# Attention stage of a four-layer graph network: another layout, ring depth and engine for the split values, masks computed in an earlier stage

## The reference

```python
h = x @ W
x_i = h[dst]; x_j = h[src]
alpha = x_i @ wa[:c] + edge_attr @ wa[c:c + ce] + x_j @ wa[c + ce:]
alpha = where(alpha > 0, alpha, 0.2 * alpha)
m = segment_max(alpha, dst)
a = exp(alpha - m[dst])
a = a / (segment_sum(a, dst)[dst] + 1e-16)
out = segment_sum(a[:, None] * x_j, dst) + bias
```

## Time and profile before

| | before |
|---|---|
| median of the runs | 3592.72 us |
| profiled execution | 3591.77 us, span 3590.0 us |
| PE, busy | 2911.7 us, 81% |
| VectorE (DVE), busy | 2904.2 us, 81% |
| ScalarE (ACT), busy | 2219.8 us, 62% |
| GpSimd (POOL), busy | 1584.4 us, 44% |
| stage of the passes | about 1241 to 1712 us of the span |
| attention stage | from about 2682 us; values from 2721.0 to 3571.6 us |
| last instruction group | output stores at 3582 us |

### The profile page before, as it was taken

How to read it: one execution, slowest core, us unless ns; L and a number is a source line. 1 busy time by engine, 2 the same in 40 slices (tenths; PEclk the granted TensorE clock), 3 DMA queues, 4 the chain that set the end, 5 groups by cost and what they waited for, 6 DMA issues and landing times.

```text
span 3590.0 us, 122167 instructions
## 1 busy us (share of the span) xinstructions
PE 2911.7 (81%) x50473; PEld 2637.4 (73%) x50473; DVE 2904.2 (81%) x4610; ACT 2219.8 (62%) x6003; POOL 1584.4 (44%) x1253
## 2 busy tenths in 40 slices
PE   0199999999999699899688888787768888888886
PEld 0178888888888599899677777777757777777775
DVE  7599999999999522233688888898857999999997
ACT  6334444444444400001698888898857898899887
POOL 2012222222221000000399988898964655666564
PEclk9999999999999899999899999999977888888887
DMA  8157777777777799898687877787738888888884
GB/s 221 66 157 244 237 232 234 243 237 231 234 243 236 253 370 360 330 328 320 215 279 259 264 264 248 254 271 250 257 124 302 279 278 277 276 290 274 267 278 129
DMA packets 606666, 907.43 MB, mean 253 GB/s; under 512 B 358505, under 2 KB 494858, under 8 KB 587163
## 3 DMA queue, kind: packets, MB, share of 16 engines
q1 hardware_dynamic: 583992, 800.62, 68.1%
q10 hardware_dynamic: 19763, 94.38, 7.1%
q0 software_dynamic: 2352, 4.52, 0.3%
HBM read 651.96 MB, written 247.40 MB: 251 GB/s over the span
## 4 chain that ended last, share of the span: by engine, by line
PE 36%; DVE 27%; ACT 14%; issue 10%; POOL 6%; DMA 5%; ACTq 1%; SPq 0%; DVEq 0%; POOLq 0%
PE ps L683 9%; PE ps L1047 8%; PE ps L709 4%; DMA U<-AD 4%; ACT U L1627 3%; POOL EDG L1268 3%; DVE EDG L1755 3%; DVE U L1817 3%; PE ps L696 3%; ACT U L569 3%; POOL EDG L1260 2%; ACT U L1329 2%; PE ps L667 2%; PE ps L1289 1%; DVE A L1389 1%
## 5 line engine op out<-in xcount | busy, mean ns | idle before, releaser
L569 ACT ACTIVATE U<-ps 128x512 bf16<-128x512 f32 (+1 forms) x637 | 356.4, 573 | 499.5 <-PE ps L696 475.5
L1627 ACT ACTIVATE U<-U,T 128x65 f32<-128x65 f32 x1806 | 460.1, 343 | 47.7 <-PE ps L1688 42.3
L1260 POOL TENSOR_TENSOR EDG<-U,edge 128x512 f32<-128x512 f32 (+1 forms) x196 | 214.3, 1098 | 584.1 <-DVE edge L1412 551.1
L1047 PE MATMUL ps<-U 128*128 128x192 bf16 x4802 | 418.5, 248 | 33.2 <-DMA U<-AD 32.8
L1047 PEld LDWEIGHTS ps<-U 128*128 128x128 bf16 x4802 | 402.8, 98 | 42.5 <-DMA U<-AD 39.2
L1655 POOL TENSOR_TENSOR U<-U 128x455 f32<-128x455 f32 x258 | 296.4, 1152 | 215.3 <-DVE U L1817 215.3
L866 DVE TENSOR_TENSOR EDG<-edge,EDG 128x1792 bf16<-128x1792 bf16 x343 | 367.5, 1083 | 14.4 <-DMA OSD<-EDG 12.0
L502 POOL DMA_INDIRECT U<-REC,nod x49 | 94.0, 1918 | 622.4 <-PE ps L638 501.2
L683 PE MATMUL ps<-U 128*128 128x98 bf16 (+1 forms) x5292 | 363.5, 223 | 4.5 <-DVE U L854 3.5
L709 PE MATMUL ps<-EDG,U 128*128 128x193 bf16 x2401 | 311.4, 249 | 51.1 <-ACT U L569 39.9
L683 PEld LDWEIGHTS ps<-U 128*128 128x128 bf16 x5292 | 341.3, 98 | 15.7 <-DVE U L854 11.9
(11 more groups left out here) (323 smaller groups left out, 7019.4 us busy)
## 6 DMA issues: line engine op xcount, KB each, us to landing
U<-ROWS SPq DMA_DIRECT2D x411, 448.0 KB, 4.7
U<-AD SPq DMA_DIRECT2D x98, 1568.0 KB, 8.6
OND<-EDG SPq DMA_DIRECT2D x343, 224.0 KB, 2.8
OSD<-EDG SPq DMA_DIRECT2D x343, 224.0 KB, 3.6
AD<-U ACTq DMA_DIRECT2D x49, 1568.0 KB, 5.6
EDG<-ROWS SPq DMA_DIRECT2D x171, 448.0 KB, 6.3
U<-OND SPq DMA_DIRECT2D x303, 224.0 KB, 5.9
U<-OSD SPq DMA_DIRECT2D x213, 224.0 KB, 4.7
```

The costliest lines, as they stand in the source:

```text
L569: ev4.by(act.activation(prow[i % NPW][:, P * g:P * (g + m)], ps[4 + gg % 2][:, 0:P * m], ACT.Copy))
L1047: ins = pe.matmul(ps[q][:, 0:192], arow[r][:, P * j:P * j + P], (XsB if p else XsA)[:, j, :, :].rearrange("p s f -> p (s f)"), start=(j == ...
L1260: ins = pool.tensor_tensor(VD[:, v:v + w, 0, KA * D:G * D].rearrange("p w (k f) -> p w k f", f=D), W_, bc(c_.unsqueeze(3), [P, w, G - KA, ...
L1627: ins = act.activation(V4[k % NV][:, 0, c, :], H[k % NHR][:, c, :], ACT.Copy, scale=a4[d % 2][:, s:s + 1])
```

## The change

The ring of values becomes one tile of NV = 6 slots. In a slot the fp32 values stand 8 bytes apart: word 0 holds the value, word 1 the remainder, and the third term is written as bf16 over the lower half of word 1. PE then reads three neighbouring halves of each pair of words. The remainder (second term) is made by GpSimd at offset 17, and the third by VectorE at offset 18; ACT and PE keep their offsets. `GV` and `GR` are empty, so all groups take this way. The one-hots are loaded at offset 5, not 3, into a ring that still has 17 buffers. The masks no longer come from the attention stage: GpSimd makes them for all blocks during the passes and SP stores them to DRAM (MSK) in the second pass; the attention stage loads the two masks of a block in bf16 at offset 2, and PE's second small transpose (L1709) becomes a bf16 product. PE's transpose L1695, ACT's copy L1613 and GpSimd's four instructions per block go.

```diff
+        msk_ok, msk_d = on(rec_t, NB), on(rank_ok, 2 * NB)
+        def passes_pool(pool):
+            msk_d.by(pool.memset(mdif[:, :, 0:1], 1.0))
+            msk_d.by(pool.memset(mdif[:, :, P:P + 1], 1.0))
+            pool.wait_ge(msk_ld.at, msk_ld.o + 16)
+            for g in range(NGB):
...
+                msk_d.by(pool.tensor_tensor(mdif[:, :, 1:P], mdst[:, bl, 1:P], mdst[:, bl, 0:P - 1], ALU.subtract))
+                pool.wait_ge(msk_d.at, msk_d.o + 4 * g + 3)
+                msk_d.by(pool.tensor_scalar(mdif, mdif, 0.0, 1.0, ALU.is_equal, ALU.subtract))
+                pool.wait_ge(msk_d.at, msk_d.o + 4 * g + 4)
+                msk_ok.by(pool.tensor_scalar(mboth[:, bl, 0, :], mdif[:, :, 0:P], BIG, None, ALU.mult))
+                msk_ok.by(pool.tensor_scalar(mboth[:, bl, 1, :], mdif[:, :, 1:P + 1], -1.0, None, ALU.mult))
+            pool.wait_ge(msk_st.at, msk_st.o + 16 * NGB)
         def passes_sp(sp):
+            msk_ld.by(sp.dma_start(mdst, ROWS3[1].rearrange("d (s r) -> s d r", r=P)), 16)
...
+                    if p and i % GB == GB - 1:
+                        g = i // GB
+                        sp.wait_ge(msk_ok.at, msk_ok.o + 2 * g + 2)
+                        msk_st.by(sp.dma_start(MSK[GB * g:GB * g + GB].rearrange("d s m r -> s d (m r)"),
+                                               mboth[:, GB * g:GB * g + GB, :, :].rearrange("p d m r -> p d (m r)")), 16)
...
-        NV = 4
-        vparts = [part(o4 + 1365 * i, 1365) for i in range(NV - 1)] + [MISC[:, 0:1365]]
-        V4 = [v.rearrange("p (s k f) -> p s k f", s=3, f=65) for v in vparts]
+        NV, NE = 6, G * 65
+        VR = part(o4, NV * NE * 2).rearrange("p (v e w) -> p v e w", v=NV, w=2)
+        VS = part(o4, NV * NE * 2).bitcast(BF16).rearrange("p (v e h) -> p v e h", v=NV, h=4)
...
+            def run_masks(d):
+                if d >= 2:
+                    sp.wait_ge(ytr.at, ytr.o + d - 1)
+                mk_ld[d % 2].by(sp.dma_start(masks[d % 2], MSK[d]), 16)
...
-                _, _, k = due4(t, 3)
+                _, _, k = due4(t, 5)
                 if k is not None:
                     hots(k)
+                d = block4(t, 2)
+                if d is not None and d >= 2:
+                    run_masks(d)
...
-                        ins = act.activation(V4[k % NV][:, 0, c, :], H[k % NHR][:, c, :], ACT.Copy, scale=a4[d % 2][:, s:s + 1])
+                        ins = act.activation(VR[:, k % NV, 65 * c:65 * c + 65, 0], H[k % NHR][:, c, :], ACT.Copy, scale=a4[d % 2][:, s:s + 1])
...
-                d, g, k = due4(t, 18)
+                d, g, k = due4(t, 17)
                 if k is not None:
-                    pool.wait_ge(rok.at, rok.o + k + 1)
-                    look.by(pool.tensor_tensor(V4[k % NV][:, 2, :, :], V4[k % NV][:, 1, :, :], S4[k % NV][:, 1, :, :], ALU.subtract))
+                    value_at(pool, k)
+                    rok.by(pool.tensor_tensor(VR[:, k % NV, :, 1], VR[:, k % NV, :, 0], VS[:, k % NV, :, 1], ALU.subtract))
...
-                        ins = pe.matmul(ps[6 + d % 2][:, 0:195], ODn[k % NOD][:, c, :], S4[k % NV][:, :, c, :],
+                        ins = pe.matmul(ps[6 + d % 2][:, 0:195], ODn[k % NOD][:, c, :], VS[:, k % NV, 65 * c:65 * c + 65, 1:4],
...
-                d, g, k = due4(t, 17)
+                d, g, k = due4(t, 18)
                 if k is not None:
-                    dve.wait_ge(vok.at, vok.o + k + 1)
-                    rok.by(dve.tensor_tensor(V4[k % NV][:, 1, :, :], V4[k % NV][:, 0, :, :], S4[k % NV][:, 0, :, :], ALU.subtract))
+                    dve.wait_ge(rok.at, rok.o + k + 1)
+                    look.by(dve.tensor_tensor(VS[:, k % NV, :, 2], VR[:, k % NV, :, 1], VS[:, k % NV, :, 3], ALU.subtract))
...
-                    dve.wait_ge(flg.at, flg.o + 2 * d + 2)
-                    dvf.by(dve.tensor_tensor_scan(ysc, negs, ps[2][0:NB, 0:P], -BIG, ALU.add, ALU.max))
+                    dve.wait_ge(mk_ld[d % 2].at, mk_ld[d % 2].o + 16 * (d // 2 + 1))
+                    dvf.by(dve.tensor_tensor_scan(ysc, masks[d % 2][:, 0, :], ps[2][0:NB, 0:P], -BIG, ALU.add, ALU.max))
```

More of the change, by code:

```diff
@@ L81, in gnn_kernel @@
         ENDS = dram("ENDS", (2, EP), I32)
+        MSK = dram("MSK", (NB, NB, 2, P), BF16)
         U = sb("U", [P, 20800])
@@ L989, in due_steps @@
             return (done if i % GB == 0 and done >= 1 else None), (i - GB if i >= GB else None)
+        msk_ld, msk_st = on(rw_st[0], 32 * ((NB + 1) // 2)), on(rw_st[1], 32 * (NB // 2))
+        msk_ok, msk_d = on(rec_t, NB), on(rank_ok, 2 * NB)
+        mdst = EDG[0:NB, 0:3136].bitcast(BF16)[:, 0:NB * P].rearrange("p (d r) -> p d r", r=P)
+        mboth = EDG[0:NB, 3136:9408].bitcast(BF16).rearrange("p (d m r) -> p d m r", m=2, r=P)
+        mdif = U[0:NB, upper + NB * 96:upper + NB * 96 + GB * 129].rearrange("p (d r) -> p d r", r=129)
+        def passes_pool(pool):
[3 more added lines that the diff above has]
+            for g in range(NGB):
+                bl = slice(GB * g, GB * g + GB)
+                if g:
+                    pool.wait_ge(msk_ok.at, msk_ok.o + 2 * g)
+                    msk_d.by(pool.memset(mdif[:, :, 0:1], 1.0))
+                    msk_d.by(pool.memset(mdif[:, :, P:P + 1], 1.0))
+                msk_d.by(pool.tensor_tensor(mdif[:, :, 1:P], mdst[:, bl, 1:P], mdst[:, bl, 0:P - 1], ALU.subtract))
[5 more added lines that the diff above has]
+            pool.wait_ge(msk_st.at, msk_st.o + 16 * NGB)
         def passes_sp(sp):
+            msk_ld.by(sp.dma_start(mdst, ROWS3[1].rearrange("d (s r) -> s d r", r=P)), 16)
             for p in range(2):
@@ L1239, in pairs3_sp @@
             sp.wait_ge(row_mm.at, 2 * NB)
+            sp.wait_ge(msk_st.at, msk_st.o + 16 * NGB)
             for n in range(4):
@@ L1472, in gnn_kernel @@
         o4 = NHR * G * 65
-        NV = 4
-        vparts = [part(o4 + 1365 * i, 1365) for i in range(NV - 1)] + [MISC[:, 0:1365]]
-        V4 = [v.rearrange("p (s k f) -> p s k f", s=3, f=65) for v in vparts]
-        S4 = [v.bitcast(BF16).rearrange("p (s k f h) -> p s k f h", s=3, f=65, h=2)[:, :, :, :, 1] for v in vparts]
-        o4 += 1365 * (NV - 1)
+        NV, NE = 6, G * 65
+        VR = part(o4, NV * NE * 2).rearrange("p (v e w) -> p v e w", v=NV, w=2)
+        VS = part(o4, NV * NE * 2).bitcast(BF16).rearrange("p (v e h) -> p v e h", v=NV, h=4)
+        o4 += NV * NE * 2
         NA4 = 14
         a4o = NA4 * W
-        odp = [part(o4 + 448 * i, 448) for i in range(15)] + [Aflat[:, a4o + 1792:a4o + 2240], Tflat[:, 2700:3148]]
-        o4 += 15 * 448
+        odp = [part(o4 + 448 * i, 448) for i in range(11)] + [Aflat[:, a4o + 1792:a4o + 2240], Tflat[:, 2700:3148], Tflat[:, 1225:1673]] \
+            + [MISC[:, 448 * i:448 * i + 448] for i in range(3)]
+        o4 += 11 * 448
         NOD = len(odp)
@@ L1496, in cell @@
             return rows[k // 2 % n][:, e:e + P]
-        seg, negs, lastf, ylast = (Tflat[0:NB, 1225 + 130 * n:1225 + 130 * n + w] for n, w in enumerate((129, P, P, P)))
+        ylast = Tflat[0:NB, 2267:2267 + P]
+        masks = [MISC[0:NB, 1365 + P * i:1365 + P * i + P].bitcast(BF16).rearrange("p (m r) -> p m r", m=2) for i in range(2)]
+        identh = ident[0:NB, 0:NB].bitcast(BF16).rearrange("p (r h) -> p r h", h=2)[:, :, 1]
         ysc = ps[3][0:NB, P:2 * P]
@@ L1516, in gnn_kernel @@
         hg, hev = on(r_used, NG), on(pj_t, NB)
-        dtr, dcp, flg, sgk = on(cat_t, NB), on(cat_ev, NB), on(cat_d, NB), on(t_out, NB)
+        mk_ld = [on(ad_st[0], 16 * ((NB + 1) // 2)), on(ad_st[1], 16 * (NB // 2))]
+        vop, rop = on(cat_t, NB), on(cat_ev, NB)
         zok, ztr, ylok, ytr = on(coef, NB), on(coll, NB), on(p3_t, NB), on(p3_ev, NB)
@@ L1533, in due4, with value_at, rest_at @@
             return (k // G, k % G, k) if 0 <= k < NT else (None, None, None)
+        GV, GR = (), ()
+        def value_at(eng, k):
+            d, g = k // G, k % G
+            if g in GV:
+                eng.wait_ge(vop.at, vop.o + d * len(GV) + GV.index(g) + 1)
+            else:
+                eng.wait_ge(vok.at, vok.o + d * (G - len(GV)) + sum(h not in GV for h in range(g + 1)))
+        def rest_at(eng, k):
+            d, g = k // G, k % G
+            if g in GR:
+                eng.wait_ge(rop.at, rop.o + d * len(GR) + GR.index(g) + 1)
+            else:
+                eng.wait_ge(rok.at, rok.o + d * (G - len(GR)) + sum(h not in GR for h in range(g + 1)))
         def block4(t, off):
@@ L1607, in pairs4_act @@
                                           ps[k % 2][:, 0:65 * G].rearrange("p (k f) -> p k f", f=65), ACT.Copy))
[L1608 to L1613, removed]
                 d = block4(t, 16)
@@ L1618, in pairs4_act @@
                 d, g, k = due4(t, 16)
-                if k is not None:
+                if k is not None and g not in GV:
                     act.wait_ge(exo.at, exo.o + d + 1)
@@ L1708, in pairs4_pe @@
                     pe.transpose(ps[3][:, 0:NB], ylast, ident[0:NB, 0:NB])
```

(9 more changed lines are left out.)

30 lines of the change are left out of this document (4 added, 26 removed).

## The result

The change made the kernel slower: 3697.53 us (3696.82 to 3701.08) against 3592.56, a ratio of 1.0294 (95% interval 1.0276 to 1.0312), where 3550 us was forecast with a range up to 3604. The profiled execution has a span of 3699.0 us.

A forecast was written before the change was run, and what follows sets the result against it. No engine was full; VectorE came nearest, lengthened by GpSimd collisions, with ACT waiting for ring slots. Terms -20 - 35 + 5 + 3 + 4 = -43 took 3591.8 to 3549, forecast as 3550 us, range 3512 to 3604.

The forecast's parts named there:

- Values 8 bytes apart: Attention stage, all engines' accesses to the values: 8-byte steps cost 0; upper end 0.37 us per group, 125 us in all.
- The stride rival: VectorE's third term: 8 bytes cost what 16 do, 125 us more, 3675 us, range 3594 to 3680; chance 0.10.
- no row has 8 bytes: Claim that no profile row showed accesses 8 bytes apart, so their price was taken from other steps.
- Ring of six: ACT's wait for PE to free a value slot goes (60.6 us), of which -20 us counts; bounds 0 to 25.8.
- no longer reaches ACT: PE's gather by target and the wait ahead of it, under 4 us together, stop delaying ACT with six slots.
- Masks: Masks leave the attention stage: less stretch of VectorE, -35 us (bounds 0 and 60); making them in the passes, +4.
- Exchange: GpSimd and VectorE swap subtractions: VectorE's new wait for GpSimd costs +5 us; PE's direct wait for VectorE costs nothing.
- One-hots: Loaded two steps later in the attention stage: PE waits in perhaps a quarter of blocks, +3 us, bounds 0 to 25.
- the cover of 1.9 us: VectorE first uses PE's one-hot product 1.9 us after it ends, so PE's wait for late one-hots is hidden.

The follow-up runs named there:

- the list of forms: Single instructions of 455 elements appended behind the kernel before's last work, each engine alone; VectorE took 1170 ns for bf16 written 8 bytes apart, 632 dense.
- the run with whole words written: The changed kernel with VectorE's third term written as an fp32 word 8 bytes apart in place of a bf16 half: 3619.9 us.
- the run of later one-hots: The kernel before with one number changed, one-hots loaded at offset 5 instead of 3: 3618.9 us, ratio 1.009.
- the two runs without the slow write on VectorE: The changed kernel with VectorE writing whole fp32 words, 3619.9 us; and the changed kernel with the exchange taken back, one-hots at offset 5, 3622.3 us.

## Why the prediction was wrong

In a row of kernels that differ by one part each: before 3589; masks 3574 (-16); interleaved at ring four 3598 (+24); ring six 3591 (-7); one-hots later 3622 (+31); exchange, which takes the slow write from GpSimd to VectorE, 3697 (+75, or about 70 by the ratios, as the kernel before ran at 3592.6 us beside the changed one). Another order of the parts gives them other sizes, as the last point shows.

- **Values 8 bytes apart** is the step that failed. I priced reads and writes together at 0 with an upper end of 0.37 us, and for writes I leaned on a memset of fp32 words 260 bytes apart. No row had a bf16 half written alone, and such a write costs 1170 - 632 = 0.54 us per group on VectorE: more than my upper end, and from an operand that I had excluded. The stride rival came nearest with 3675 us (up to 3680), but on the ground of the step between operands; that it came near is in part luck. The reads were indeed free on VectorE (632 ns), as the rule on two hits per line in the Trainium skill, SBUF — State Buffer (section on door 1), says; the rule as I used it says nothing of the size of a written piece.
- The rows for that step were misread as well. L1809, called dense, reads its operand in PSUM 8 bytes apart (`g4[:, :, 0]`), so "no row has 8 bytes" is wrong; and L1852 writes its result 16 bytes apart too, so its 246 ns don't say whether reading or writing costs them.
- PE's operand, taken at 0, costs 20 ns a product in the list of forms, which is 48 us of busy time over the 2401 in the stage, and GpSimd's third term 1.20 us for 0.945. With both, and VectorE spared, the layout costs 24 us. How the 24 divide between them was not tried.
- **Ring of six**: -20 forecast, -7 measured (-4 by the ratios). The step that failed is "no longer reaches ACT": ACT's next wait, for PE's gather, was only 5.8 us in the kernel before (line below, 2800 to 3500 us) because the ring's wait stood in front of it. With four and six slots it is 10.7 and 81.0 us in 850.

```profile
ACT U L1606 <- PE ps L1668: 5.8, 7, 1.9
```

- **Masks**: -35 + 4 forecast, -16 measured. VectorE's busy time fell by the 35, but two of its waits grew by 26 over the same window, and the stretch of the values became shorter by 26 us only. The step that failed is that busy time taken from VectorE was counted in full as time. The values also begin 9 us later. In the passes the last product begins at 1718.0 us in this kernel, at 1711.4 before the change and at 1712.7 after it, in the run with whole words written 1708.7, and in the run of later one-hots, which has no masks there, 1706.5. Single traces scatter by more than the 4 us, so this term is neither confirmed nor refuted. GpSimd's work on the masks took 69.5 us, not 35, and was done by 1320 us, where it cost nothing that shows.
- **Exchange**: +5 forecast, +21 measured alone. The wait for GpSimd was sized rightly; PE's direct wait for VectorE, called nothing, is 42.8 us in 700 (46.5 with the fourth buffer) where its wait for GpSimd was 15.7.
- **One-hots**: +3 forecast with an end at 25, +30 measured. The mechanism stood in the text. The mis-sized terms are how often PE waits (28 times in 700 us, about 39 blocks, not a quarter) and the cover of 1.9 us, read from one block; the landing's median rose from 5.9 to 6.5 us besides.
- The order of the terms was also taken as independent: with VectorE at 919 of 953 us the one-hots cost 11 to 13 us, and 31 without the slow write; and the exchange costs 21 us alone, but nothing between the two runs without the slow write on VectorE (3620 and 3622 us).

## What to carry to other kernels

Before interleaving values to save memory, look at the smallest piece that each engine writes, not only at the step: measure the exact form by a few instructions behind a kernel. A wait for a ring is worth little to remove (80 us of waiting here, 4 to 7 us of time) while the next instruction of the queue waits for the same late engine; name that next wait first. A load that is issued later must be held against the latest of its landings in many blocks, not the median in one.

## What the runs showed of the hardware

- VectorE's subtraction of 455 elements: bf16 halves written 8 bytes apart 1170 to 1208 ns, 4 bytes apart 668, fp32 words 8 bytes apart 634, dense 632. GpSimd, same list: 1202 to 1208, 1146, 1143 and 1142 ns.
- GpSimd's subtraction with an fp32 result takes 945 ns when both operands lie in the same words, and 1142 when they lie in two tiles, both dense; with both 8 bytes apart in two tiles 1342. So for GpSimd reads 8 bytes apart are not free in two tiles.
- PE's product over 195 moving columns takes 95 ns with a step of 4 bytes and 115 with three neighbouring halves out of four, at a granted clock of 1.00.
